# Layer-norm moments of x computed by loaded part, routing of two chunks per pass, and routing instructions moved within VectorE's step

## The reference, cut to what matters

```python
x = x + xattn(layernorm(x), ctx)              # each sequence attends to its own context and itself
h = layernorm(x)                              # moments of x + xattn
x_mix = h + sigmoid(r) * wkv(k, v) @ Wo       # time mixing, a scan along the sequence
ei = layernorm(x_mix) * g2 + b2
probs = softmax(ei @ router_w); vals, idx = top_k(probs, 2)
x = x + h_mix + moe(ei, idx)                  # 8 experts, 2 per token
x = x + ffn(layernorm(x))                     # shared GEGLU plus 1 of 8 experts
```

## Time and profile before

| what | us |
|---|---|
| three timed runs, median (lowest to highest) | 969.79 (968.96 to 971.59) |
| the profiled execution, device time | 966.43 |
| its span in the trace | 964.7 |
| busy in the span: PE / DVE / POOL / ACT | 858.3 / 445.0 / 349.3 / 316.3 |
| mean granted TensorE clock | 0.953 of full |

### The profile page before, as it was taken

The page is one execution under the profiler, slowest core; times in us unless marked ns, Lnnn a source line. Parts: engine busy times, 40 slices in busy tenths (PEclk is TensorE's granted clock), DMA queues, the critical chain, the costliest instruction groups (busy, mean ns, idle before and its releaser), DMA issues. The chain is left out here.

```text
span 964.7 us, 19179 instructions
## 1 busy us (share of the span) xinstructions
PE 858.3 (89%) x6306; PEld 768.6 (80%) x6306; DVE 445.0 (46%) x1253; ACT 316.3 (33%) x712; POOL 349.3 (36%) x605
## 2 busy tenths in 40 slices
PE   5899989886667999999949999968999999999994
PEld 4567766665566889999849999957999999999993
DVE  1279989888774555555523333353111111111113
ACT  1466767664542445555411111100111111111110
POOL 1445677766775355544142222211100010000006
PEclk9899999998688989999979999989999999999998
DMA  9875557534612322263121111102998988999716
GB/s 355 277 268 189 194 112 233 155 103 188 169 43 53 79 67 83 83 214 84 50 66 33 34 38 40 38 28 73 336 330 305 329 301 324 303 319 306 270 61 175
DMA packets 92096, 161.79 MB, mean 168 GB/s; under 512 B 13832, under 2 KB 71112, under 8 KB 88680
## 3 DMA queue, kind: packets, MB, share of 16 engines
q1 hardware_dynamic: 71008, 103.39, 32.2%
q10 hardware_dynamic: 12832, 37.82, 10.5%
q0 software_dynamic: 8176, 19.57, 7.9%
HBM read 146.10 MB, written 14.66 MB: 167 GB/s over the span
## 5 line engine op out<-in xcount | busy, mean ns | idle before, releaser
L1691 PEld LDWEIGHTS bank<-zT_f,we 128*128 128x128 f32 x1472 | 167.9, 192 | 1.8 <-ACT zT_f L1979 0.7
L1691 PE MATMUL bank<-zT_f,we 128*128 128x128 f32 x1472 | 168.2, 275 | 0.5 <-ACT zT_f L1979 0.5
L1708 DVE TENSOR_TENSOR hT_f<-bank,act_g 128x512 f32<-128x512 f32 x78 | 53.8, 691 | 227.6 <-PE bank L1691 208.0
L1700 ACT ACTIVATE act_g<-bank 128x512 f32<-128x512 f32 x78 | 46.6, 597 | 320.4 <-PE bank L1691 320.4
L1691 PE MATMUL bank<-zT_c,a_x 128*128 128x128 f32 x1024 | 121.4, 281 | 0.3 <-PEq L1521 0.3
L1691 PEld LDWEIGHTS bank<-zT_c,a_x 128*128 128x128 f32 x1024 | 119.2, 197 | 0.8 <-issue 0.7
L361 POOL DMA_INDIRECT arena_a<-rows_e,pick x78 | 76.0, 975 | 29.8 <-issue 29.8
L410 PE MATMUL bank<-arena_b,arena_a 128*128 128x128 f32 x624 | 81.8, 288 | 1.6 <-DVE hT L546 1.6
L1715 PE MATMUL bank<-we,hT_f 128*128 128x256 f32 x368 | 83.2, 379 | 0.0
L410 PEld LDWEIGHTS bank<-arena_b,arena_a 128*128 128x128 f32 x624 | 78.2, 204 | 2.4 <-DVE arena_b L538 2.4
L1715 PEld LDWEIGHTS bank<-we,hT_f 128*128 128x128 f32 x368 | 68.1, 190 | 8.3
(11 more groups left out here) (273 smaller groups left out, 1361.8 us busy)
## 6 DMA issues: line engine op xcount, KB each, us to landing
we<-in_W_dram SPq DMA_DIRECT2D x69, 1024.0 KB, 7.4
arena_a<-in_ctx_n_dram ACTq DMA_DIRECT2D x16, 1152.0 KB, 7.2
arena_a<-in_ctx_t_dram SPq DMA_DIRECT2D x16, 1028.0 KB, 9.0
rows_y<-arena_a ACTq DMA_DIRECT2D x39, 128.0 KB, 1.7
arena_a<-in_w_moe_dram ACTq DMA_DIRECT2D x3, 1156.0 KB, 5.3
arena_a<-in_w_moe_dram ACTq DMA_DIRECT2D x3, 1152.0 KB, 7.5
rows_f<-yr ACTq DMA_DIRECT2D x23, 128.0 KB, 6.3
rows_e<-arena_b SPq DMA_DIRECT2D x64, 32.0 KB, 4.0
```

Of the source, the lines that this page charges most:

```text
L1691: last = nc.tensor.matmul(bank[half][:, f * P:(f + 1) * P], w12[:, i, k, col0:col0 + P], zT[:, k], start=k == 0, stop=k == KD - 1)
L1700: nc.scalar.activation(act_g[:, half], bU[half][:], ACT.Gelu).then_inc(self.ac_g, 1)
L1708: nc.vector.tensor_tensor(hT[:, parity, half * HH:(half + 1) * HH].rearrange("p f t -> p (f t)"), bG[half][:], act_g[:, half], ALU.mult).t ...
```

## The change

Moments. `stats0` and `rstd0` take a part of x instead of a chunk: VectorE makes the moments of all its chunks in one go, and GpSimd four instructions for the part instead of three for each chunk. Part 0 is done ahead of the steps and part 1 (chunks 1 to 3) at the start of step 0. `STATS_AT` puts part 2 at the end of step 2, part 3 at the end of step 4, part 4 at the end of step 5, on VectorE behind `largest_score`, on GpSimd behind `rstd1` and ahead of `routing_constants`. SyncE issues the loads of parts 3 and 4 in steps 2 and 3, behind the keys' load of the step (before: in steps 2 and 5, ahead of it).

Routing. `largest` and `largest_at` still run in each step, but `largest` stands behind `denominator` instead of ahead of `value_sum`. `one_hot`, `both`, `own_rank`, `sum_rank`, `slots`, `ranks` and `count` run for two chunks at once, in the steps in which h is odd (9, 11, ... 23). `both` stands one drain later; `own_rank`, `sum_rank` and `slots` stand at the end of the step, around `mixed`, with one drain more. On TensorE `ranks` stands behind `values` instead of ahead of `attended`. `list_tokens` follows one step later for even chunks, and lists two chunks in steps 16 and 24 and none in steps 9 and 17.

VectorE's `attended(b)` also moves: it stands ahead of `moments1(c)`, behind which it stood.

```diff
+        STATS_AT = {2: 2, 4: 3, 5: 4}
...
-                if n in (5, 8):
-                    load_x(3 if n == 5 else 4)
                 if n < G:
                     load_keys(n)
+                if s in (2, 3):
+                    load_x(s + 1)
...
-            def rstd0(n):
...
+            def rstd0(i):
+                lo, hi = X_PARTS[i]
+                v, r, m = (rs0[:, j, lo:hi] for j in range(3))
+                pool.wait_ge(dv_st0, i + 1)
+                nc.gpsimd.tensor_scalar(v, mv0[:, lo:hi, 1], EPS, None, ALU.add).then_inc(po_v0, 1)
+                pool.wait_ge(po_v0, i + 1)
+                nc.gpsimd.tensor_tensor(r, v, eps_pow[:].to_broadcast([P, hi - lo]), ALU.pow).then_inc(po_p0, 1)
+                pool.wait_ge(po_p0, i + 1)
+                nc.gpsimd.tensor_scalar(m, mv0[:, lo:hi, 0], -1.0, None, ALU.mult).then_inc(po_n0, 1)
+                pool.wait_ge(po_n0, i + 1)
+                nc.gpsimd.tensor_tensor(m, m, r, ALU.mult).then_inc(po_r0, 1)
...
-            def count(n):
-                pool.wait_ge(dv_mask, n + 1)
-                need(pool, pe_rank, n)
-                need(pool, po_sum, n)
-                if n > CUT:
+            def count(q):
+                pool.wait_ge(dv_mask, q + 1)
+                need(pool, pe_rank, q)
+                if q > CUT // 2:
                     pool.wait_ge(pe_tot_a, 1)
-                nc.gpsimd.tensor_tensor(earlier[:, (n + 1) % 2], earlier[:, n % 2], mask[:, n % 2], ALU.add).then_inc(po_sum, 1)
+                nc.gpsimd.tensor_tensor(earlier[:, 2], earlier[:, q % 2], mask[:, 0], ALU.add).then_inc(po_sum, 1)
+                pool.wait_ge(po_sum, 2 * q + 1)
+                nc.gpsimd.tensor_tensor(earlier[:, (q + 1) % 2], earlier[:, 2], mask[:, 1], ALU.add).then_inc(po_sum, 1)
 
...
+            def listed_at(i):
+                at_once = (CUT - 1, G - 1)
+                if i % 2:
+                    return (i - 1, i) if i in at_once else (i - 1,)
+                return () if i - 1 in at_once or i == 0 else (i - 1,)
...
-                if live(s + 1) is not None:
-                    rstd0(s + 1)
+                if s == 0:
+                    rstd0(1)
                 if w is not None:
                     numerator(w)
                 if i is not None:
-                    list_tokens(i)
+                    for n in listed_at(i):
+                        list_tokens(n)
                 if g is not None:
                     normed(g)
-                if h is not None:
-                    count(h)
+                if h is not None and h % 2:
+                    count(h // 2)
                 if a is not None:
                     with_bias(a)
                 if x is not None:
                     rstd3(x)
                 if c is not None:
                     rstd1(c)
+                if s in STATS_AT:
+                    rstd0(STATS_AT[s])
                 if s == 1:
                     time_mix_constants()
                 if s == 2:
...
-            def ranks(n):
-                pe.wait_ge(dv_mask, n + 1)
...
+            def ranks(q):
+                pe.wait_ge(dv_mask, q + 1)
+                need(pe, po_sum, 2 * q)
+                need(pe, dv_prod, q)
+                upto(dv_dk, pe, 2 * q + 6)
+                two, odd = bK[:, D:D + 2 * E], bK[:, D + E:D + 2 * E]
+                nc.tensor.matmul(two, before_m[:], mask[:].rearrange("p c e -> p (c e)"), start=True, stop=False)
+                nc.tensor.matmul(bK[:, D:D + E], ones_m[:], earlier[:, q % 2], start=False, stop=False)
+                nc.tensor.matmul(odd, ones_m[:], earlier[:, q % 2], start=False, stop=False)
+                nc.tensor.matmul(odd, ones_m[:], mask[:, 0], start=False, stop=True).then_inc(pe_rank, 1)
+
+            def totals_a():
+                need(pe, po_sum, CUT)
+                need(pe, dv_prod, CUT // 2)
+                upto(dv_dk, pe, CUT + 5)
+                nc.tensor.matmul(bK[:, D + E:D + 2 * E], ones_m[:], earlier[:, CUT // 2 % 2], start=True, stop=True).then_inc(pe_tot_a, 1)
 
...
                     values(k)
+                if h == CUT:
+                    totals_a()
+                if h is not None and h % 2:
+                    ranks(h // 2)
+                if k is not None:
...
-            def stats0(n):
-                part = [i for i, (lo, hi) in enumerate(X_PARTS) if lo <= n < hi][0]
-                dve.wait_ge(ld_x[part], 16)
-                nc.vector.bn_stats(st0[:, n % 2], xz[:, n])
-
-            def moments0(n):
-                nc.vector.bn_aggr(mv0[:, n % 2], st0[:, n % 2]).then_inc(dv_st0, 1)
+            def stats0(i):
+                lo, hi = X_PARTS[i]
+                dve.wait_ge(ld_x[i], 16)
+                for n in range(lo, hi):
+                    nc.vector.bn_stats(st0[:, n % 4], xz[:, n])
+                dve.drain()
+                for n in range(lo, hi):
+                    last = nc.vector.bn_aggr(mv0[:, n], st0[:, n % 4])
+                last.then_inc(dv_st0, 1)
 
...
+            def one_hot(q):
+                nc.vector.tensor_tensor(hot[:, 2 * q:2 * q + 2], iota_e[:].unsqueeze(1).unsqueeze(1).to_broadcast([P, 2, 2, E]),
+                                        top_at[:, :, 0:2].unsqueeze(3).to_broadcast([P, 2, 2, E]), ALU.is_equal)
+
+            def both(q):
+                need(dve, pe_rank, q)
+                need(dve, po_sum, 2 * q)
+                two = hot[:, 2 * q:2 * q + 2]
+                nc.vector.tensor_tensor(mask[:], two[:, :, 0], two[:, :, 1], ALU.add).then_inc(dv_mask, 1)
+
+            def own_rank(q):
+                dve.wait_ge(pe_rank, q + 1)
+                ranks = bK[:, D:D + 2 * E].rearrange("p (c e) -> p c e", e=E)
+                nc.vector.tensor_tensor(hot_rank[:], hot[:, 2 * q:2 * q + 2], ranks.unsqueeze(2).to_broadcast([P, 2, 2, E]),
                                         ALU.mult).then_inc(dv_prod, 1)
 
-            def sum_rank(n):
+            def sum_rank():
                 nc.vector.reduce_sum(rank[:], hot_rank[:], AX)
 
-            def slots(n):
-                nc.vector.scalar_tensor_tensor(listed[:, n], top_at[:, n % 2, 0:2], float(TOK), rank[:],
+            def slots(q):
+                nc.vector.scalar_tensor_tensor(listed[:, 2 * q:2 * q + 2], top_at[:, :, 0:2], float(TOK), rank[:],
                                                ALU.mult, ALU.add).then_inc(dv_slot, 1)
 
...
-                a, b, c, t = live(s), live(s - 1), live(s - 2), live(s + 1)
+                a, b, c = live(s), live(s - 1), live(s - 2)
+                if s == 0:
+                    stats0(1)
                 z, k, w, x, h = (live(s - LAG - i) for i in (0, 1, 2, 3, 5))
+                q = h // 2 if h is not None and h % 2 else None
                 if w is not None:
                     decayed(w)
-                if t is not None:
-                    stats0(t)
                 dve.drain()
                 if w is not None:
                     weight_sum(w)
-                if t is not None:
-                    moments0(t)
-                if h is not None:
-                    largest(h)
-                if w is not None:
                     value_sum(w)
                 dve.drain()
-                if h is not None:
-                    largest_at(h)
                 if w is not None:
                     new_value(w)
                     denominator(w)
-                dve.drain()
                 if h is not None:
-                    one_hot(h)
+                    largest(h)
+                dve.drain()
+                if h is not None:
+                    largest_at(h)
                 if k is not None:
                     running_max(k)
                 dve.drain()
-                if h is not None:
-                    both(h)
+                if q is not None:
+                    one_hot(q)
                 if k is not None:
                     key_rise(k)
                 if x is not None:
...
                 if w is not None:
                     gated(w)
                 dve.drain()
+                if q is not None:
+                    both(q)
                 if x is not None:
                     stats3(x)
                 if w is not None:
...
                     moments3(x)
                 if c is not None:
                     residual_att(c)
-                if h is not None:
-                    own_rank(h)
                 dve.drain()
                 if c is not None:
                     stats1(c)
-                if h is not None:
-                    sum_rank(h)
+                if b is not None:
+                    attended(b)
                 dve.drain()
                 if c is not None:
                     moments1(c)
-                if h is not None:
-                    slots(h)
-                if b is not None:
-                    attended(b)
                 if z is not None:
                     change(z)
                 if w is not None:
                     quotient(w)
                 if a is not None:
```

(11 more changed lines are left out.)

60 lines of the change are left out of this document (17 added, 43 removed).

## The result

The changed kernel takes 979.49 us (median of 4 runs, 976.45 to 982.15) where the kernel before takes 969.38 (4 runs): 1.0096 times as long, 95% interval 1.0073 to 1.0118. Measured again beside other kernels it was 1.0087 (1.0072 to 1.0101). So it is 8 to 9 us slower. The forecast was 971.7, with 978 as the upper end of its range. Two launches of a later measurement, one of them of the kernel before, took 2.2 ms; medians and ratios leave them out.

What follows compares the result with a forecast made beforehand. The prediction took the mix stage to be bound by VectorE and its waits and the last stage by TensorE. Its terms summed to +1.9 us on the profiled 966.43, 968.3, or 971.7 in terms of the median; range 963 to 978.

Steps and rivals of the forecast that it cites:

- step 3: Mix stage, step 3: constants wait behind the batch, +3.4 us, and moments1 moves behind attended, about 0.8; +4.2 in all.
- routing, MAX8, lists (steps 9 to 24): Terms of routing and order from step 9 on, -5.3 us in sum, with 0 for steps 20 to 24.
- step 9: Step 9 has no list yet and is held only by own_value's wait for residual_att: +1.5 us.
- steps 10 to 15: Three pairs of steps take 82.5 us against 85.2 before: -2.7 us (-6 to +1).
- The term of steps 18 and 19: Step 18 loses MAX8's wait and five instructions, -2.3 us; step 19 shortens VectorE's wait for ScalarE, -1.3 us.
- slower: Rival: the 3.6 us of steps 18 and 19 do not reach the tiles: +5.5, 975.3 us; slower cases 0.30.
- The constants behind the batch: Step 3: GpSimd's routing constants wait behind part 2's moments, so ScalarE's scaled_in and TensorE's attended start later: +3.4 us.
- The batches: Ends of steps 4 and 5: VectorE's moments batches of 1.9 us each, less 0.4 in step 5: +3.4 us (2 to 4).
- The pairs of steps: Steps 10 to 15: even steps 12.1 us, odd steps 15.4, as own_rank waits 2 us for TensorE's ranks.
- The start: Step 0: two more stats, two more aggregates and GpSimd's fourth instruction, hidden by nothing: +1.2 us.
- The rule of the Trainium skill: Rival: VectorE's pipe empties between instructions, each small one removed saving 0.16 us, not 0.08: -1.3, 968.5 us; chance 0.03.
- the loop that the prediction described: Steps 10 to 15: MAX8, new_value, GpSimd's numerator, rs_2 and the logits form a 14.2 us loop, which moving MAX8 opens.

Runs made afterwards that it cites:

- experiment 12: The kernel before with VectorE's attended ahead of moments1 and nothing else: 971.90 us, 1.0054 of the kernel before.
- 4: The changed kernel with moments of x by single chunks again, batches and moved loads undone: 970.42 us, 1.0045 of the kernel before.
- experiment 5: The changed kernel with moments by single chunks again and moments1 ahead of attended: 966.11 us, 0.9995 of the kernel before.
- 1: The changed kernel with GpSimd's routing constants ahead of the batch of step 2: 972.44 us, 1.0055 of the kernel before.
- 3: The changed kernel with the constants ahead of step 2's batch and moments1 ahead of attended: 967.57 us, 1.0010 of the kernel before.
- 2: The changed kernel with moments1 ahead of attended again in every step: 972.70 us, 1.0061 of the kernel before.
- experiment 7: The kernel before with the moments of x by parts alone, loads of x included: 974.88 us, 1.0071 of the kernel before.
- experiment 13: The kernel before with moments by parts and GpSimd's constants ahead of step 2's batch: 966.85 us, 0.9996 of the kernel before.
- experiment 8: The kernel before with only the lists of tokens at the change's later places: 966.50 us, 0.9985 of the kernel before.
- experiment 10: Experiment 9's kernel with the lists of tokens behind the gather in steps 18 to 23: 956.31 us, 0.9903 of the kernel before.
- experiment 9: The changed kernel with single-chunk moments, moments1 ahead of attended, and own_rank, sum_rank and slots behind mixed: 959.65 us, 0.9933 of the kernel before.
- experiment 11: The kernel before with MAX8 alone moved behind denominator, one drain more: 959.85 us, 0.9934 of the kernel before.

## Why the prediction was wrong

**The step that failed** is one half-sentence of step 3: "Moments1 also moves behind attended, so rs_2, hidden(4) and the next out_T come later by about 0.8". Step 4, where it should have shown, lost 2.9 us in both profiles of the changed kernel, and alone on the kernel before the swap costs 5 us (experiment 12). Two things were missing. I priced the swap in one step by VectorE's own spacing, while it applies in every step, and in the early ones rs_2 ends a chain on which TensorE waits; in step 3 moments1 inherited the very wait of 3.04 us that I had just put ahead of attended. And I let TensorE run its matmuls at the durations of the earlier trace rows, while behind some of its pauses query_key takes 3.2 to 3.8 us, not 2.05. The cost of the order is shown by pairs of runs that differ in it alone: 12 against the kernel before, 4 against 5, 1 against 3, each 4 to 5 us; the changed kernel against 2, where the clock fell elsewhere instead, gives 2.5 to 3.4. That the clock is a part of it is read from their rows (1.7 of 2.95 us in step 4 of experiment 12); no run changed the clock alone. It would also explain why experiments 1 and 2 gained little singly and 8 us together. The direction of the sum was right, its size a fifth.

Set beside the experiments, the sum had three parts:

| part | forecast | measured alone |
|---|---|---|
| moments by parts (start, constants, batches, steps 6 to 8) | +6.4 | +6.9 (experiment 7) |
| moments1 behind attended | +0.8 | +5.2 (experiment 12) |
| routing, MAX8, lists (steps 9 to 24) | -5.3 | -0.5 (experiment 5) |
| sum | +1.9 | +11.6; the whole change is +8 to 9 |

Together the parts cost less than their sum, and why was not tested. So the swap is one of two terms that failed, and the gain of the routing is the other, of the same size. That the first part came out so well is in part luck: experiment 13 has it without the wait for the constants at 0, where the sum would leave 3. In experiment 5 the rows had -3.2 of the -5.3 at step 20, and most of that is gone at the end; where it went stays open. The pieces that fell short by the rows are step 9 (+2.4, forecast +1.5), steps 10 to 15 (-1.8, forecast -2.7) and step 19.

**The term of steps 18 and 19** was mis-sized by about 1 us in the changed kernel: step 18 gained 2.69 (forecast 2.3), step 19 nothing (1.3), and 0.9 to 3.8 were lost again by the tile map. That fits the rival "slower" in part: norm_out waits for GpSimd. The extra list alone does not cost it, as experiment 8 shows on the kernel before. The order within GpSimd's step is part of it: behind the gather, the lists cost 3 us less (experiment 10 against 9). Why the first profile lost 2.9 us more here than the second stays open.

**What held.** The constants behind the batch: +3.5 measured, +3.4 forecast, and the two places named for it (4.88 us idle before scaled_in, four statistics in a row) are in the trace. The batches: 3.1 and 4.3, forecast 3.4. The pairs of steps: 12.1 and 15.3 us, forecast 12.1 and 15.4, with the stall at own_rank put down to ranks (1.58 us where I had 2). The start: 1.2 and 2.55, forecast 1.2. GpSimd's power over four columns took 1.04 us where one column takes 0.57, which I had left out; GpSimd's four instructions of the batch took 1.9 us up to the constants where the sum had 1.7. The rule of the Trainium skill on VectorE's drain (VectorE: DVE Perf Modes, section The DRAIN you can't avoid) would have made the sum lower, further from the result, and the steps of 12.1 us bear out the smaller price. The prediction gave it short. That section of the Trainium skill adds that a next instruction starts earlier where nothing holds it, so the 0.08 us need not go against it; its advice to minimise the count stands in another section, Rules for kernel authors.

**What I undervalued** is the part of the change that works. MAX8's move alone is 6.4 us faster (experiment 11), by the loop that the prediction described. In the changed kernel that gain is used up by own_rank's stall, about 6 us (experiment 9 against 5), which the routing of two chunks brings, before the early steps are counted. The pairs without their stall and MAX8 alone come to the same, 0.9933 and 0.9934, so no run shows that routing two chunks at once earns anything of its own on this kernel; at the tile map it is 2.7 us ahead, and with the lists behind the gather the ratios are 0.9903 and 0.9922, with intervals that overlap.
